# A small copy behind every indirect DMA of GpSimd: key columns written one at a time, and one element copied behind each gather

## What is computed

```python
# layer one: edge features (200,000 x 128) projected and summed by source node
edge_proj = edge_attr @ W_sum + b_sum
sum3d = jax.ops.segment_sum(edge_proj, src, num_segments=num_nodes)
return x + z_in[in_deg] + z_out[out_deg] + cent_term + vor_term + sum3d

# layer two: rows of the nodes gathered by source, summed by destination
agg = jax.ops.segment_sum(x[src], dst, num_segments=N)
mean = agg / jnp.maximum(deg, 1.0)[:, None]
out = mean @ W_l.T + b_l + x @ W_r.T
```

## Time and profile before

| | |
|---|---|
| median of 2 runs | 5826.15 us (5824.57 to 5827.73) |
| the profiled execution | 5827.4 us |
| POOL busy | 3633.3 us, 62% of the span, 3833 instructions |
| DVE busy | 3398.3 us, 58% |
| PE busy | 3771.0 us, 65% |
| mean granted TensorE clock | 0.861 of full speed |

### The profile page before, as it was taken

How to read it: one execution, slowest core, us unless ns; L and a number is a source line. 1 busy time by engine, 2 the same in 40 slices (tenths; PEclk the granted TensorE clock), 3 DMA queues, 4 the chain that set the end, 5 groups by cost and what they waited for, 6 DMA issues and landing times. The chain is left out here.

```text
span 5827.4 us, 55903 instructions
## 1 busy us (share of the span) xinstructions
PE 3771.0 (65%) x15976; PEld 2734.7 (47%) x15976; DVE 3398.3 (58%) x6459; ACT 749.7 (13%) x1759; POOL 3633.3 (62%) x3833
## 2 busy tenths in 40 slices
PE   0006666479319914789967777776666666546995
PEld 0002222236219914668844444444444444336884
DVE  8989999864618814662445665654333333376223
ACT  8300000143100000032310000000000000022331
POOL 1777777777876676601157777777777777501552
PEclk9999999999659967999987788778877888667997
DMA  4333333333349946600043333333333333621225
GB/s 113 99 100 101 107 102 102 107 100 102 90 150 378 379 143 203 213 18 1 17 119 104 105 105 104 104 104 106 106 106 106 106 106 106 74 88 44 72 72 171
DMA packets 594577, 675.30 MB, mean 116 GB/s; under 512 B 215966, under 2 KB 449496, under 8 KB 594034
## 3 DMA queue, kind: packets, MB, share of 16 engines
q0 software_dynamic: 145440, 364.03, 21.7%
q1 hardware_dynamic: 346606, 200.47, 12.7%
q10 hardware_dynamic: 102244, 107.43, 5.4%
HBM read 531.94 MB, written 139.66 MB: 115 GB/s over the span
## 5 line engine op out<-in xcount | busy, mean ns | idle before, releaser
L1711 POOL DMA_INDIRECT rows<-projected_rows,pw_in x1664 | 1592.3, 957 | 576.7 <-issue 487.4
L1960 PE MATMUL pg<-rows,hot 128*125 128x256 f32 x3328 | 1171.3, 489 | 641.4 <-DVE hot L1800 361.9
L635 POOL DMA_INDIRECT rows_by_src_a<-ring,pos_src x1216 | 1210.6, 996 | 353.5 <-issue 336.9
L1960 PEld LDWEIGHTS pg<-rows,hot 128*125 128x125 f32 x3328 | 722.1, 236 | 1063.1 <-DVE hot L1800 531.4
L1726 DVE TENSOR_TENSOR agg<-agg,pg 125x256 f32 x832 | 349.3, 420 | 1056.2 <-PE pg L1960 1047.7
L986 PE MATMUL pqkv<-hots 128*126 128x450 bf16 x1042 | 458.3, 595 | 205.9 <-DVE hots L664 205.9
L1081 PE MATMUL pqkv<-hots,XT 128*128 128x125 f32 x3024 | 341.1, 276 | 219.7 <-DVE hots L880 219.6
L1081 PEld LDWEIGHTS pqkv<-hots,XT 128*128 128x128 f32 x3024 | 340.4, 193 | 220.6 <-DVE hots L880 220.4
L635 POOL DMA_INDIRECT rows_by_src_b<-ring,pos_src x347 | 354.4, 1021 | 101.0 <-issue 96.0
L986 PEld LDWEIGHTS pqkv<-hots 128*126 128x126 bf16 x1042 | 193.5, 216 | 471.5 <-DVE hots L664 395.4
L1800 DVE SCALAR_TENSOR_TENSOR hot<-pw_in,m_block_first,g_numbers 128x250 f32<-128x250 int32 x832 | 391.1, 470 | 38.6 <-DMA m_wn<-in_L_gnn_W_r 15.4
(11 more groups left out here) (442 smaller groups left out, 6170.6 us busy)
## 6 DMA issues: line engine op xcount, KB each, us to landing
ring<-in_edge_attr SPq DMA_DIRECT2D x142, 704.0 KB
XT<-rows_by_src_a ACTq DMA_DIRECT2D x252, 387.0 KB, 6.6
win<-rows_by_src_b SPq DMA_DIRECT2D x112, 387.0 KB, 4.1
rows<-projected_rows,pw_in POOLq DMA_INDIRECT x1664, 2.7
rows_by_src_a<-ring,pos_src POOLq DMA_INDIRECT x1216
XT<-moe_results SPq DMA_DIRECT2D x25, 448.0 KB
e_w<-in_L_ffn_W SPq DMA_DIRECT2D x16, 512.0 KB
pw_in<-pairs_by_dst SPq DMA_DIRECT2D x432, 2.0 KB
```

The source lines that it names most:

```text
L635: pool.indirect_dma_start(rows_a_d if c < CA else rows_b_d, bass.IndirectOffsetOnAxis(ap=pos_src[:, c:c + 1].bitcast(U32), axis=0), ring4[ ...
L1711: pool.indirect_dma_start(rows[:, (2 * (s % RU) + r) * D:(2 * (s % RU) + r + 1) * D], None, proj_d, bass.IndirectOffsetOnAxis(ap=pairs_of( ...
L1960: mm = pe.matmul(pg[0:P, s % 4, 0:D], hot[:, ((s % 4) * 2 + r) * P:((s % 4) * 2 + r + 1) * P], rows[:, (2 * (s % RU) + r) * D:(2 * (s % RU ...
```

## The change

The keys are no longer copied 11 columns at once ahead of a unit. The copies of the first unit's 11 columns stand ahead of the first scatter, and then behind the scatter of column c follows the copy of the key of column c + 11. The wait for a unit's load goes with the first of its columns. In layer two a copy of one element (`ident[0:1, 0:1]`, a float, to a bf16 number) follows each gather; each writes a cell of its own in a new tile `g_src_now` that nothing reads, in partition 0, 32, 64 or 96.

```diff
-            def put_keys(n):
-
-                h, count = n % RINGS, min(HC, EF + 1 - n * HC)
-                two_loads = n == UNITS - 1 and count > 1
-                pool.wait_ge(ring_in[h], 16 * (n // RINGS + 1 + two_loads))
-                pool.tensor_copy(ring4[:, h, 0:count, ED], pair_w[:, n * HC:n * HC + count, 0]).then_inc(keys_put, 1)
+            def put_key(c):
+
+                n, j = divmod(c, HC)
+                h = n % RINGS
+                if j == 0:
+                    two_loads = n == UNITS - 1 and EF + 1 - n * HC > 1
+                    pool.wait_ge(ring_in[h], 16 * (n // RINGS + 1 + two_loads))
+                pool.tensor_copy(ring4[:, h, j, ED:ED + 1], pair_w[:, c, 0:1]).then_inc(keys_put, 1)
 
             pool.wait_ge(ranked, 1)
-            put_keys(0)
+            for c in range(HC):
+                put_key(c)
             for n in range(UNITS):
-                if n + 1 < UNITS:
-                    put_keys(n + 1)
-                pool.wait_ge(keys_put, n + 1)
+                pool.wait_ge(keys_put, min((n + 1) * HC, EF + 1))
                 for c in range(n * HC, min((n + 1) * HC, EF + 1)):
...
                                             ring4[:, n % RINGS, c - n * HC, :], None).then_inc(ring_out[n % RINGS], 16)
+                    if c + HC <= EF:
+                        put_key(c + HC)
...
+        src_now = sbuf(ctx, "g_src_now", [128, NW2 // 2], BF16)
...
                                                 ).then_inc(rows_in[s % RU], 16)
+                        pool.tensor_copy(src_now[s % 2 * 64 + r * 32:s % 2 * 64 + r * 32 + 1, (i * U + s) // 2:(i * U + s) // 2 + 1], ident[0:1, 0:1])
```

## The result

The changed kernel is slower: 6117.17 us (median of two runs, 6106.91 to 6127.44) against 5826.15 us, a ratio of 1.0493 with a 95% interval of 1.0476 to 1.0511. The profiled execution took 6125.4 us where that of before took 5827.4, so there are 298 us to place.

What follows compares the result with a forecast made beforehand. The prediction took POOL's loops of scatters and gathers to bound the kernel. Its terms, 99 + 36 + 18 - 27 + 100 = 226 us on 5827, gave 6053, say 6050 us, with a range of 5860 to 6140.

Steps and rivals of the forecast that it cites:

- POOL sets the pace: Scatter and gather loops: POOL waits for TensorE only 23.5 us; a microsecond added to its loop adds to the span.
- A copy between scatters: Scatters: 1.34 us start to start, not 1.27; 0.07 us for each of 1,420 added copies, 99 us.
- Collisions: Scatters: copies stretched by VectorE, 71 us if all new, nothing if stalls only move; half taken, +36 us.
- Seams: Scatters, unit starts: waiting for the key copy right ahead costs 0.13 us, 142 times, 18 us.
- Ring waits: Scatters: POOL's 13 waits for loads of edge rows, 48.7 us, each shrink by about 2.1 us, -27 us.
- Layer two: Gathers: 1,664 one-element copies of 0.20 us, each adding 0.06 us from gather to gather, 100 us.
- The hidden copy: Rival, chance 0.15: copies run beside the DMA, the next DMA skips its 0.30 us; gathers -233 us, 5720 or about 5500.
- The cheap copy: Rival, chance 0.18: a one-element copy takes 0.10 to 0.15 us; layer two -67 to +17 us, total 5886 to 5970.
- the stretched one: Rival, chance 0.07: every copy costs its stretched mean, 0.261 us; scatters 188, layer two 200, total 6215 us.

Runs made afterwards that it cites:

- the experiment: Scatters' half of the change alone, a unit's first scatter not waiting for the key copied right ahead, against the kernel before: 5939.02 us, ratio 1.018.
- the memsets: Kernel before, with a memset of one bf16 element behind each gather in layer two, writing the cells the change's copies write: 5833.11 us, ratio 1.0002.

## Why the prediction was right, and which terms were off

The direction, the bound and the mechanism held: 6117 us against 6050 forecast, inside 5860 to 6140, and every microsecond in the two loops of POOL that were named. Term by term:

**POOL sets the pace.** Right. In the gathers 27.1 us are put down to waiting for TensorE, 23.5 before, but these are 178 gathers with 0.15 us each ahead of them and never more than 0.2, what stands ahead of every gather: after the change POOL doesn't wait for TensorE at all. VectorE's waits grew with it (after the change, to be held against the earlier trace rows):

```profile
DVE agg L1731 <- PE pg L1965: 1219.1, 698, 4.5
...
DVE hots L883 <- DMA XT<-rows_by_src_a: 267.0, 32, 246.6
...
DVE hot L1178 <- DMA win<-rows_by_src_b: 185.8, 4, 184.4
```

The first sorted window is waited for 246.6 us instead of 140.4, 106 us more; the last of the first 1,216 scatters starts 108.8 us later (1819.2 against 1710.4 in the trace of before).

**A copy between scatters, 0.07 us.** Right. The steady row is 0.98 + 0.19 + 0.16 = 1.33 to 1.34 us, against 1.27; 1420 x 0.067 = 95 us, forecast 99. Two rows of copies of before were enough to price 1,420.

**Collisions, 36 us.** The copies' busy time is 354.8 us, of which 1563 x 0.192 (their median) = 300 would be undisturbed, so 55 us are stretched, against 7 us before. The scatters are stretched by as much as before, 52 against 54 us (mean less median, times their number). So about 46 us are new: the stalls of the copies came on top, two thirds of the full 71 us and not half. The Trainium skill (SBUF — State Buffer, "SBUF: two separate sides") states that where an operation of VectorE and one of GpSimd both need the shared port pair, whichever comes second is blocked until the other has ended. The prediction read from it that a stall would only move from a scatter to a copy, which would give nothing new, and that reading the 46 us don't bear out; the rule itself these rows don't test. Why the stalls came on top is not shown. POOL is at work in more of the time and may meet more of VectorE's operations.

**Seams, 18 us.** Right: 17 us by the rows, and 16.8 us less idle time ahead of the scatters in the experiment.

**Ring waits, -27 us.** Right: 48.7 fell to 19.8 us, -29, where kernels with the scatters of before have 41.0 to 48.7 us. Alone it may be worth less in time than in waiting: with the wide copy behind the first scatter 16 us of waiting went, and the times told no gain apart.

Sum for the scatters: 95 + 46 + 17 - 29 = 129 us, forecast 126, measured 124.6. That the forecast came within 2 us is luck in part, since its terms were off by 4 and 10 us against each other.

**Layer two, 100 us.** This term was mis-sized: 174 us by the stage, 163 us in time. The step was "0.20 + 0.15 - 0.30 + 0.01 = 0.06 us". Measured: the gather 0.967 us, 0.020 more than its 0.947 of before, not 0.01; then 0.043 us ahead of the copy, not in the sum at all; the copy 0.182 us, not 0.20; 0.155 us behind it. Together 0.020 + 0.043 + 0.182 + 0.155 - 0.303 = 0.097 us, x 1664 = 162 us, and 12 us more for copies that took longer than the median (mean 0.189, median 0.182). No row of before could show the 0.043 us, since all its copies wrote the same 128 partitions. Without it, as in the kernels that keep to one partition, the stage is 95 to 98 us longer (84 to 86 us in time), and the forecast of 100 would have held, with a copy taken 0.02 us too dear and the DMA behind it 0.01 too cheap.

**The rivals.** The hidden copy is out: even a copy in one partition begins only when the DMA has ended, and the next DMA 0.15 us behind the copy. The Trainium skill (GPSIMD Engine Reference, "Instruction dispatch") lets each core go on by itself. No run here shows that with a DMA ahead or behind: the memsets, which read nothing and of which three in four write partition 32, 64 or 96, began 0.03 to 0.05 us behind the gather's end all the same. The overlap of two copies, 0.05 us, does not bear on it, since both write the same partition. A copy that also reads away from partition 0 was not tried. The cheap copy is out as well: 0.18 us for one element, 0.20 for 128. So is the stretched one: the copies average 0.227 us in the scatters and 0.189 in the gathers, not 0.261.

## What to carry to other kernels

An idle gap that stands behind each instruction of a kind is not room: ask what may run in it and how long, and price it by the distance from start to start with and without a filler. Here 0.09 us of work was free in a gap of 0.30 us and 0.18 us was paid, because the next DMA came 0.15 us behind the filler's end, and took 0.02 us longer itself. Merge small operations on the engine that sets the pace rather than spread them. And where a change mixes a gain with its costs, take the gain alone and as far as it goes: a wait moved later by nine scatters was worth 0.8% here, by one scatter nothing that the times tell.

## What the runs showed that was not expected

- One-element copies of GpSimd to partitions 0, 32, 64 and 96 in turn each begin 0.04 us later than copies that all write one partition or all 128.
- Copies added in layer two made the scatters of layer one 0.007 us shorter each (median 0.960 against 0.967 us), though nothing in that stage was changed. The cause is open.
- The DMA behind a copy is itself 0.02 us longer (0.967 against 0.947 us); behind a memset it is not.
- TensorE's granted clock in the gathers fell from 0.78 to 0.72 of full speed while it did the same 4,336 matmuls with more idle time between. The stage of the kernel after the change (length, then PE, PEld, DVE, ACT, POOL, clock, DMA share, GB/s):

```profile
3076.00:5353.00 2277.00, 1575.05 (x4336) 1030.94 (x4336) 1013.59 (x2367) 64.82 (x152) 1946.89 (x3327) 0.72 0.38 97
```

  Its busy time rose by 120 us against the earlier trace rows, and none of that reached the span, since TensorE is not what POOL waits for. A mean of 0.72 lies between the two levels of 1.2 and 2.4 GHz: it spent more of the stage at the lower one.
